# Token sums of the last two pairs read the odd tile in PSUM, and GpSimd's low parts wait for the second norm

## The reference

```python
res = hidden_states
h = rmsnorm(hidden_states, ln1_w)
h = res + mamba2(h, ...)          # "the scan": scores, decays, y, out projection
res = h
h2 = rmsnorm(h, ln2_w)            # second norm
mlp = silu(h2 @ gate_w.T) * (h2 @ up_w.T) @ down_w.T   # INTER = 1792
return res + mlp
```

## Time and profile before

| | us |
|---|---|
| median of 3 runs | 395.52 (395.28 to 396.03) |
| the profiled execution | 395.84 |
| its span, first to last instruction | 394.0 |
| PE busy | 378.9 (96%) |
| DVE busy | 294.9 (75%) |
| ACT busy | 190.2 (48%) |
| POOL busy | 134.4 (34%) |
| granted TensorE clock, mean | 0.995 |

### The profile page before, as it was taken

How to read it: one execution, slowest core, us unless ns; L and a number is a source line. 1 busy time by engine, 2 the same in 40 slices (tenths; PEclk the granted TensorE clock), 3 DMA queues, 4 the chain that set the end, 5 groups by cost and what they waited for, 6 DMA issues and landing times.

```text
span 394.0 us, 5136 instructions
## 1 busy us (share of the span) xinstructions
PE 378.9 (96%) x1795; PEld 303.5 (77%) x1795; DVE 294.9 (75%) x514; ACT 190.2 (48%) x385; POOL 134.4 (34%) x121
## 2 busy tenths in 40 slices
PE   7999999999989999999999999999999999998994
PEld 3778787766767888888888888878788888896773
DVE  2599995289989767979797978695555856758487
ACT  5778456877774634242424334863324144142241
POOL 2504222855857422828374646920000000000000
PEclk8999999999999999999999999999999999999999
DMA  7901530110001043021111111441110102101002
GB/s 253 327 12 54 184 124 15 53 55 0 1 2 55 2 151 114 25 84 52 56 53 54 56 53 53 161 161 53 55 48 35 53 28 80 53 27 53 28 2 80
DMA packets 12978, 27.62 MB, mean 70 GB/s; under 512 B 1841, under 2 KB 2225, under 8 KB 12954
## 3 DMA queue, kind: packets, MB, share of 16 engines
q1 hardware_dynamic: 12090, 25.87, 19.7%
q10 hardware_dynamic: 864, 1.44, 1.0%
HBM read 25.20 MB, written 2.11 MB: 69 GB/s over the span
## 4 chain that ended last, share of the span: by engine, by line
PE 81%; DVE 11%; issue 2%; POOL 2%; ACT 1%; DMA 1%; SPq 0%; DVEq 0%; ACTq 0%; POOLq 0%
PE bank L648 24%; PE bank L650 23%; PE bank L649 23%; PE bank L900 2%; PE bank L911 2%; DMA rows<-x 1%; PE bank L710 1%; DVE tmp L1614 1%; DVE tmp L1801 1%; PE bank L687 1%; PE bank L719 1%; DVE station L1584 1%; DVE tmp L1609 1%; DVE sets_f L1598 1%; PE bank L916 1%
## 5 line engine op out<-in xcount | busy, mean ns | idle before, releaser
L648 PE MATMUL bank<-sets,station 128*128 128x512 f32 x392 | 158.9, 405 | 0.9 <-POOL station L508 0.9
L650 PE MATMUL bank<-sets,station 128*128 128x512 f32 x392 | 152.9, 390 | 0.0
L649 PE MATMUL bank<-sets,station 128*128 128x512 f32 x392 | 152.9, 390 | 0.0
L648 PEld LDWEIGHTS bank<-sets,station 128*128 128x128 f32 x392 | 73.7, 188 | 17.9 <-issue 2.5
L649 PEld LDWEIGHTS bank<-sets,station 128*128 128x128 f32 x392 | 73.8, 188 | 16.0 <-issue 2.2
L650 PEld LDWEIGHTS bank<-sets,station 128*128 128x128 f32 x392 | 73.6, 188 | 15.8
L606 POOL TENSOR_TENSOR big<-tmp,side_f 128x512 f32<-128x512 f32 x17 | 26.4, 1567 | 24.8 <-DVE side_f L1674 24.8
L1362 ACT ACTIVATE small<-small 128x1 f32<-128x1 f32 x24 | 7.1, 295 | 50.0 <-DVE small L1803 50.0
L508 POOL TENSOR_TENSOR station<-raw,station 128x1024 fp32r<-128x1024 f32 x7 | 16.7, 2391 | 40.1 <-ACT station L1053 40.1
L1674 DVE TENSOR_TENSOR side_f<-side_f,bank 128x512 f32<-128x512 f32 x36 | 24.6, 684 | 4.5 <-PE bank L650 4.2
L1522 DVE SCALAR_TENSOR_TENSOR big<-bank,cw,big 128x508 f32<-128x508 f32 (+2 forms) x36 | 26.2, 739 | 1.3 <-ACT big L1113 0.3
(11 more groups left out here) (206 smaller groups left out, 661.3 us busy)
## 6 DMA issues: line engine op xcount, KB each, us to landing
raw<-wstream SPq DMA_DIRECT2D x31, 512.0 KB, 3.7
rows<-x SPq DMA_DIRECT2D x8, 256.0 KB, 5.0
big<-ctxT SPq DMA_DIRECT2D x8, 256.0 KB, 2.6
big<-ctx SPq DMA_DIRECT2D x8, 256.0 KB, 3.0
out<-tmp ACTq DMA_DIRECT2D x5, 256.0 KB, 2.0
decays<-step_rows SPq DMA_DIRECT2D x4, 256.0 KB, 3.7
big<-step_rows SPq DMA_DIRECT2D x4, 256.0 KB, 5.4
out<-tmp SPq DMA_DIRECT2D x2, 256.0 KB, 2.1
```

The source lines that it names most:

```text
L648: pe.matmul(ps, a_hi, b_lo, start=first, stop=False)
L649: pe.matmul(ps, a_hi, b_hi, start=False, stop=False)
L650: return pe.matmul(ps, a_lo, b_hi, start=False, stop=last)
```

## The change

- The token sums of pairs 2 and 3 take the odd tile (5 or 7) from its PSUM bank instead of an fp32 copy in SBUF, so ACT's copies of the tiles 5 and 7 go. T3 is made last but one, as T2 - b11 from SBUF, instead of b22 - b12: of a pair's four sums two read PSUM.
- The pairs' order of work becomes 0, 2, 1, 3 (`SUMS_ORDER`) on DVE, ACT and POOL.
- DVE's order at the end of the scan changes: `token_sums(2)` and `low_h2(6)` come ahead of `add_h(7)`; `norm2(7)` follows `add_h(7)` directly, and `token_sums(1)` comes behind it.
- POOL's `lo_part` of the last plain weight block waits for `norm2(6)` (`hn2` at 7), and `t_low(0)` for `norm2(7)` (`hn2` at 8).
- PE turns tile 7 ahead of both parts of `gate_up(1,0)`; the banks 5 and 7 are now freed by the token sums (`t_f32`), not by the copies.

```diff
+SUMS_ORDER = (0, 2, 1, 3)
...
         def h2_rows(t):
-            if t < B - 2:
-                first = T3 if t % 2 else T1
-                return sets[:, first:first + 2, 0, :, bass.ts(3 if t in (2, 3) else 2, P)]
-            return tmp[:, bass.ds((4 + t - (B - 2)) * D, D)].rearrange("p (g c q) -> p g c q", g=2, c=2)
+            if t in (B - 3, B - 1):
+                return h2_turned(t)
+            if t == B - 2:
+                return tmp[:, 4 * D:5 * D].rearrange("p (g c q) -> p g c q", g=2, c=2)
+            first = T3 if t % 2 else T1
+            return sets[:, first:first + 2, 0, :, bass.ts(2 + t // 2 % 2, P)]
...
             def t_low(i):
-                pool.wait_ge(t_hi, i + 1)
+                pool.wait_ge(t_hi, SUMS_ORDER.index(i) + 1)
...
                 if b == B:
+                    pool.wait_ge(hn2, B - 1)
                     lo_part(GU_CHUNK + 1, ringS[:, 1, 1, :], ringS[:, 1, 0, :])
-                    t_low(0)
+            pool.wait_ge(hn2, B)
+            t_low(0)
...
             weight_sums(G0)
-            for i in range(1, HB - 1):
+            for i in SUMS_ORDER[1:HB - 1]:
                 t_low(i)
...
             gate_up(0, 0, (1,))
+            turn_h2(B - 1)
             pe.wait_ge(w_lo, GU_CHUNK + 2)
-            pe.wait_ge(h2_lo, HB + 1)
-            pe.wait_ge(h2_f32, HB + 1)
-            gate_up(1, 0, (0,))
-            turn_h2(B - 1)
             pe.wait_ge(h2_lo, B - 2)
-            pe.wait_ge(h2_f32, B - 2)
-            gate_up(1, 0, (1,))
+            pe.wait_ge(t_f32, 2)
+            gate_up(1, 0)
             pe.wait_ge(h2_lo, B)
             gate_up(0, 1)
-            pe.wait_ge(h2_f32, B)
+            pe.wait_ge(t_f32, HB)
             gate_up(1, 1)
...
                     hi_of_h2(b - 3)
-                    f32_of_h2(b - 3)
+                    if b - 3 <= HB:
+                        f32_of_h2(b - 3)
...
+            hi_of_t(2)
+            hi_of_h2(B - 1)
             hi_of_t(1)
             weight_hi(G0)
-            hi_of_h2(B - 1)
-            f32_of_h2(B - 1)
-            hi_of_t(2)
             hi_of_t(HB - 1)
...
                 v.tensor_tensor(f[:, 0, :, :], b12, b11, ALU.subtract).then_inc(t_step, 1)
-                v.tensor_tensor(f[:, 2, :, :], b22, b12, ALU.subtract)
-                v.wait_ge(t_step, 2 * i - 1)
+                if i < 2:
+                    v.tensor_tensor(f[:, 2, :, :], b22, b12, ALU.subtract)
+                v.wait_ge(t_step, 2 * k - 1)
                 v.tensor_tensor(f[:, 1, :, :], b22, f[:, 0, :, :], ALU.subtract).then_inc(t_step, 1)
-                v.wait_ge(t_step, 2 * i)
+                v.wait_ge(t_step, 2 * k)
+                if i >= 2:
+                    v.tensor_tensor(f[:, 2, :, :], f[:, 1, :, :], b11, ALU.subtract)
                 v.tensor_tensor(f[:, 3, :, :], f[:, 1, :, :], b21, ALU.subtract).then_inc(t_f32, 1)
...
             for b in range(B + 2):
                 if b >= 2:
                     add_h(b - 2)
-                if b == B + 1:
-                    low_h2(B - 2)
-                    token_sums(2)
...
                 if b == B:
                     low_h2(B - 3)
                     v.wait_ge(t_f32, 1)
-                    token_sums(1)
+                    token_sums(2)
+                    low_h2(B - 2)
+            token_sums(1)
             low_h2(B - 1)
             token_sums(HB - 1)
```

More of the change, by code:

```diff
@@ L325, in h2_rows, with h2_kept @@
         def h2_rows(t):
-            if t < B - 2:
-                first = T3 if t % 2 else T1
-                return sets[:, first:first + 2, 0, :, bass.ts(3 if t in (2, 3) else 2, P)]
-            return tmp[:, bass.ds((4 + t - (B - 2)) * D, D)].rearrange("p (g c q) -> p g c q", g=2, c=2)
+            if t in (B - 3, B - 1):
[4 more added lines that the diff above has]
+            return sets[:, first:first + 2, 0, :, bass.ts(2 + t // 2 % 2, P)]
+        def h2_kept(t):
+            return t + 1 if t <= HB else HB + 2
         def score_bank(b):
@@ L1161, in hi_of_t @@
             def hi_of_t(i):
-                act.wait_ge(t_f32, i + 1)
+                act.wait_ge(t_f32, SUMS_ORDER.index(i) + 1)
                 if i >= 2:
@@ L1589, in low_h2 @@
                 v.wait_ge(h2_hi, b + 1)
-                v.wait_ge(h2_f32, b + 1)
+                if b not in (B - 3, B - 1):
+                    v.wait_ge(h2_f32, h2_kept(b))
                 v.tensor_tensor(h2_cols(b, 1), h2_turned(b), h2_cols(b, 0).bitcast(F32), ALU.subtract).then_inc(h2_lo, 1)
@@ L1596, in token_sums @@
                 b11, b21, b12, b22 = even[:, 0, :, :], even[:, 1, :, :], odd[:, 0, :, :], odd[:, 1, :, :]
-                v.wait_ge(h2_f32, 2 * i + 2)
+                k = SUMS_ORDER.index(i)
+                v.wait_ge(h2_hi, 2 * i + 2)
+                v.wait_ge(h2_f32, h2_kept(2 * i) if i >= 2 else 2 * i + 2)
                 v.tensor_tensor(f[:, 0, :, :], b12, b11, ALU.subtract).then_inc(t_step, 1)
-                v.tensor_tensor(f[:, 2, :, :], b22, b12, ALU.subtract)
-                v.wait_ge(t_step, 2 * i - 1)
+                if i < 2:
+                    v.tensor_tensor(f[:, 2, :, :], b22, b12, ALU.subtract)
+                v.wait_ge(t_step, 2 * k - 1)
                 v.tensor_tensor(f[:, 1, :, :], b22, f[:, 0, :, :], ALU.subtract).then_inc(t_step, 1)
-                v.wait_ge(t_step, 2 * i)
+                v.wait_ge(t_step, 2 * k)
+                if i >= 2:
+                    v.tensor_tensor(f[:, 2, :, :], f[:, 1, :, :], b11, ALU.subtract)
                 v.tensor_tensor(f[:, 3, :, :], f[:, 1, :, :], b21, ALU.subtract).then_inc(t_f32, 1)
```

## The result

The changed kernel takes 393.39 us (median of 10 runs, 393.03 to 395.02), the kernel before 396.08 in the runs beside it (median of 10); the ratio is 0.9927, 95% interval 0.9908 to 0.9946, that is 2.1 to 3.6 us less. The forecast was 393.0, from 392.4 to 394.3. The profiled execution took 393.21 us, its span 391.4 against 394.0.

What follows compares the result with a forecast made beforehand. PE, busy 378.9 of 394.0 us, bounds the kernel; its waits for tile norms were 2.8 us. Winning 2.02 at tile 6 and 2.51 by gate_up(0,1), 2.5 off the median 395.52 gives 393.0 us, range 392.4 to 394.3.

Steps and rivals of the forecast that it cites:

- Step 1: Norm of tile 6 on DVE: with POOL held back, 0.75 us, ending 2.02 us earlier, PE's transposes following.
- Steps 2 and 3: POOL's lo_part moves behind the norm at no cost; PE reaches gate_up(0,0)'s up part at 119.14, free for tile 7 at 121.86.
- Step 4: DVE up to the norm of tile 7: sums ahead of add_h(7) cost nothing, without room; norm ends at 122.33.
- Step 5: PE from tile 7: a new stall of 0.52 before turn_h2(7); gate_up(0,1) could start 2.51 us earlier, at 128.37.
- Step 6: Low part of tile 7 on DVE: ready at 127.77, 0.6 early, if the first sum precedes t_low(0); otherwise PE loses 0.08.
- Step 7: Pair 3's sums before gate_up(1,1) at 133.81: end near 131.6 or 133.8; second Strassen product's low part covered by 1 us.
- the worse of its two cases: Step 7, pair 3's two SBUF sums: both held by POOL low parts, ending near 133.8.

Runs made afterwards that it cites:

- x6: Changed kernel with tile 7 turned at its old place, between the parts of gate_up(1,0), whose gate_up(1,1) up part alone awaits pair 3's sums: 394.36 us, ratio 0.9920.
- x5: Changed kernel with ACT's two copies back and all four sums of pairs 2 and 3 from SBUF; order and waits as changed: 394.75 us, ratio 0.9946.
- x4: Changed kernel without POOL's second wait, so pair 0's low part follows the last residual directly: 396.84 us, ratio 1.0009.
- x2: Kernel before with POOL's first wait alone (weight block's low part behind the norm of tile 6): 397.42 us, ratio 1.0035.
- x7: x4 with ten idle matmuls in PE's queue ahead of the turn of tile 7, filling the stall: 396.33 us, ratio 0.9981.

## Why the prediction was right, point by point

- *Step 1, the norm of tile 6.* 0.75, and PE's transposes follow with no listed wait (115.68). Right; x1, with nothing but the waits, and x3, with everything but them, show that it was POOL, and nothing else of the change.
- *Steps 2 and 3.* POOL's low part started 0.08 after the norm, took 2.41 and held nothing but the third sum of step 4; PE's up part of `gate_up(0,0)` began 3.24 after the transposes (3.25 predicted).
- *Step 4.* The sums from PSUM took 0.42 (0.41 taken, 0.68 the upper bound). The third sum ended at 118.39, 0.28 after POOL's low part, as read from the earlier trace rows. `add_h(7)` came 4.38 after the start of the norm of tile 6, 4.33 predicted; the norm of tile 7 took 0.75.
- *Step 5.* PE's remaining wait is 0.41 (0.52 predicted); `gate_up(0,1)` starts 13.31 us after the norm of tile 6, 13.28 predicted, 15.79 before.
- *Step 6.* The first sum of pair 1 went ahead of POOL's low part, which then took 2.51 instead of 2.39, and the second sum was held (2.62). The low part of tile 7 ended at 127.38, 0.8 us before PE asked. This is where the Trainium skill's rule ("SBUF — State Buffer", "Who interferes with whom": the one issued first blocks the other) decided what no row of before could; the trace agrees with it on the order, for the sum began at 122.07 and POOL's low part at 122.23.
- *Step 7* came out in the worse of its two cases: both SBUF sums of pair 3 were held by a POOL low part (2.64 and 2.61) and ended at 133.38, only 0.25 before `gate_up(1,1)` needed bank 7. The forecast had a tie here (133.8 against 133.81), so that PE lost nothing was in part luck. The second Strassen product had its last low part at 139.26, 1.2 us early. Nothing was handed back.
- *The total.* From the norm of tile 6 on the gain is 2.4 us, 2.5 forecast. The forecast started from a median of 395.52; in the runs beside the changed kernel that of the kernel before was 396.08, so that the gain by medians is 2.7. That 393.39 lies so close to 393.0 is in part chance.
- *What the prediction didn't see.* It booked the whole change as one gain. The stalls go by the waits alone, with room: a norm of 0.75 behind two sets of sums is at 122.7 (x1), early enough for PE's old order, and only the early turn of tile 7 makes PE wait again (step 5's 0.52). With the early turn undone (x6) the new order and the PSUM reads add nothing to the waits: both take 275.9. With the early turn, the PSUM reads and the missing copies save 1.1 us (x5). No run has the waits and the early turn in the old order. An estimate from rows: in x1 the norm of tile 7 ends 8.70 us after that of tile 6 began, and in the changed kernel PE is free for the early turn at 6.93, so PE would stand still for some 1.8 us, where x5 shows 1.6 and the changed kernel 0.4. So the reordering and the PSUM reads mainly repair a delay that the early turn brings.

## What to carry to other kernels

A DVE instruction with two SBUF inputs that runs beside a long GpSimd instruction can be held until that one ends: here a norm took 2.77 us instead of 0.75, and a sum 2.62 instead of 0.42. Where such an instruction stands on the critical path, a wait that holds GpSimd back moves the cost to the engine that has slack. Before work is reordered, try the wait alone: here it gave 3.0 us, the whole change 2.4. And a stall removed at one place but lengthened at another isn't neutral: in x4 a stall of 2.4 us on TensorE cost 1.5 us more than its length.

## What the runs showed of the hardware

After a stall of TensorE of 2.4 us (x4) and one of 3.2 us (x2) the granted clock from 127 to 130 was 0.51 and 0.50, the lower of its two levels (1.2 GHz), and was back at 1.00 or 0.97 in the next stretch; before them the engine had worked at 1.00 without a listed wait from the turn of tile 6 on. After the stalls of 1.9 (the kernel before and x3) and 1.6 us (x5) the windows show 1.00, in this order:

```profile
118.00:124.00 6.00, 6.00 (x29) 1.00 0.25 90
```

```profile
118.00:124.00 6.00, 5.68 (x26) 1.00 0.28 88
```

```profile
127.00:130.00 3.00, 3.00 (x15) 1.00 0.00 0
```

In x4 the lower level cost 1.5 us on top of the stall, in x7 ten idle matmuls in the same place brought them back. I had expected only the stalls themselves, and two of the six first expectations (x2 and x4) failed on it. All this is read from one profiled execution of each kernel. The ten runs of x4 go from 394.94 to 398.55 us, so the clock need not have fallen in each of them, nor have stayed up in each run of the kernel before; their windows are not on record.
